# A selective-scan kernel: six of 48 drive products a step move to GpSimd, fed by DMA-broadcast B rows

## The reference, cut to what matters

```python
xs, z = split(h @ in_w)                       # 192 channels each
xc = silu(causal_conv4(xs) + conv_b)
dt, Bm, Cm = split(xc @ xproj_w)              # 6, 16 and 16 columns
delta = softplus(dt @ dt_w + dt_b)
dA  = exp(delta[..., None] * A)               # 16 states per channel
dBx = delta[..., None] * Bm[:, :, None, :] * xc[..., None]
h_t = dA_t * h_{t-1} + dBx_t                  # scan over the 4096 tokens
y = (einsum('blds,bls->bld', h, Cm) + Dp * xc) * silu(z)
seq = seq + y @ out_w
```

## Time and profile before

| | |
|---|---|
| median of 3 runs | 4664.84 us (4664.05 to 4667.70) |
| the profiled execution: its time, its span | 4665.67 us, 4663.9 us |
| first and last scan start (L600, 1536 of them) | 68.6 and 3117.8 us |
| DVE, PE, ACT, POOL busy | 3569.4, 4156.8, 2405.1, 2479.7 us |

### The profile page before, as it was taken

How to read it: one execution, slowest core, us unless ns; L and a number is a source line. 1 busy time by engine, 2 the same in 40 slices (tenths; PEclk the granted TensorE clock), 3 DMA queues, 4 the chain that set the end, 5 groups by cost and what they waited for, 6 DMA issues and landing times. The chain is left out here.

```text
span 4663.9 us, 44769 instructions
## 1 busy us (share of the span) xinstructions
PE 4156.8 (89%) x13922; PEld 1791.2 (38%) x13922; DVE 3569.4 (77%) x4331; ACT 2405.1 (52%) x3937; POOL 2479.7 (53%) x1991
## 2 busy tenths in 40 slices
PE   7999999999999999999999999863989888988964
PEld 2333333333333333333333333221546555655543
DVE  4999999999999999999999999976015415414345
ACT  5666667666666667666666666632012312312223
POOL 4778877888778877888778877761000000000000
PEclk8999999999999999999999999996999999999976
DMA  3444444444444444444444444433010010000000
GB/s 94 131 131 139 135 143 135 137 136 145 135 135 138 133 145 137 136 136 142 136 134 139 137 138 135 127 115 100 12 42 18 18 43 17 18 15 4 18 1 14
DMA packets 135434, 459.67 MB, mean 99 GB/s; under 512 B 20623, under 2 KB 23122, under 8 KB 133662
## 3 DMA queue, kind: packets, MB, share of 16 engines
q1 hardware_dynamic: 135198, 456.82, 32.0%
HBM read 431.28 MB, written 20.97 MB: 97 GB/s over the span
## 5 line engine op out<-in xcount | busy, mean ns | idle before, releaser
L668 POOL TENSOR_TENSOR prod<-states,c_rows 128x512 f32<-128x512 f32 x1536 | 1935.9, 1274 | 591.5 <-DVE states L600 575.7
L600 DVE TENSOR_TENSOR_SCAN states<-decay,carry,bpsum 128x512 f32<-128x512 f32 x1536 | 1937.6, 1262 | 0.0
L357 PE MATMUL ypsum<-prod,identity 128*128 128x512 f32 x3072 | 1587.8, 598 | 0.4 <-POOL prod L668 0.3
L459 ACT ACTIVATE decay<-delta,decay_rate 128x512 f32<-128x512 f32 x1536 | 1078.4, 716 | 722.3 <-DVE states L600 623.6
L587 DVE TENSOR_TENSOR bpsum<-bpsum,dx 128x512 f32<-128x512 f32 x1536 | 1034.8, 674 | 89.9 <-PE bpsum L350 71.7
L350 PE MATMUL bpsum<-b_rows,select 96*128 96x512 bf16 x1536 | 595.4, 388 | 163.7 <-DVE states L600 162.1
L357 PEld LDWEIGHTS ypsum<-prod,identity 128*128 128x128 f32 x3072 | 592.0, 194 | 311.3 <-issue 176.3
L350 PEld LDWEIGHTS bpsum<-b_rows,select 96*128 96x128 bf16 x1536 | 147.9, 96 | 1068.1 <-DVE states L600 666.2
L1073 PE MATMUL convp<-img_hi,w_hi 96*96 96x512 f16 (+1 forms) x1568 | 483.4, 385 | 65.1 <-PEq L1476 49.0
L1434 DVE SCALAR_TENSOR_TENSOR x<-convp,unscale,x_group 96x1024 f32<-96x1024 f32 x16 | 20.4, 1278 | 406.3 <-PE convp L1073 406.3
L1073 PE MATMUL convp<-img_hi,w_lo 128*96 128x512 f16 (+1 forms) x896 | 276.3, 388 | 0.0
(11 more groups left out here) (215 smaller groups left out, 4526.2 us busy)
## 6 DMA issues: line engine op xcount, KB each, us to landing
c_rows<-c_map SPq DMA_DIRECT2D x512, 512.0 KB, 3.7
c_rows<-c_map SPq DMA_DIRECT2D x512, 256.0 KB, 3.9
x_in<-in_x SPq DMA_DIRECT2D x16, 384.0 KB, 6.0
fused_map<-fused SPq DMA_DIRECT2D x16, 384.0 KB, 5.1
work<-fused_map SPq DMA_DIRECT2D x4, 1536.0 KB, 9.8
x<-in_x SPq DMA_DIRECT2D x4, 1536.0 KB, 16.1
x_biased_map<-work SPq DMA_DIRECT2D x4, 1536.0 KB, 7.1
x_group<-x_biased_map SPq DMA_DIRECT2D x16, 384.0 KB, 3.7
```

The source lines that it names most:

```text
L357: pe.matmul(ypsum[:, group % Y_BANKS, :], identity[:, :], prod[:, n % P_RING, :], start=s == 0, stop=s == STATES - 1).then_inc(summed, 1)
L459: act.activation(decay[:, n % RING, :], delta[k % 2][:, g, :], ACT.Exp, scale=decay_rate[:, ORDER[k][0], g, s:s + 1]).then_inc(decay_ready, 1)
L600: dve.tensor_tensor_scan(states[:, n % H_RING, :], decay[:, n % RING, :], bpsum[:, n % B_BANKS, :], carry[:, at, u:u + 1], ALU.mult, ALU.a ...
L668: pool.tensor_tensor(prod[:, n % P_RING, :], states[:, n % H_RING, :], c_rows[:, n // C_STATES % C_RING, n % C_STATES, :], ALU.mult).then_ ...
```

## The change

Six units of each step, 19, 23, 27, 31, 35 and 47, are *pooled*. For them there is no PE broadcast and no DVE scale. The B row, stored in f32 in DRAM beside C, is broadcast by a DMA on SP's queue into a ring of two SBUF buffers (`b_wide`); POOL multiplies it by dx into `drive` (two buffers) in the slot two before the unit; ACT writes the decay of that unit into the PSUM bank that the broadcast would have used, three slots ahead; the scan takes its factor from PSUM and its addend from `drive`. The projection is one chain of three matmuls (B once, C, dt). The split is made on 32 rows, and mid and low are moved to their rows of `b_rows` by two DMAs on SP. Several due slots move forward; one buffer of softplus (`tmp2`) becomes single.

```diff
+POOL_UNITS, POOL_LEAD, B_RING = (19, 23, 27, 31, 35, 47), 2, 2
 EARLY:
-    "proj": [30, 31, 32, 33, 34, 35], "hi": [35, 36], "rest": [37], "mid": [38], "low": [39],
-    "dt": [37, 40, 41], "v": [38, 41, 42], "soft": [39, 40, 41, 42, 43, 44],
+    "proj": [30, 31, 32], "hi": [33], "rest": [35], "mid": [36], "low": [37],
+    "dt": [34, 38, 36], "v": [35, 39, 37], "soft": [36, 37, 38, 39, 40, 41],
-SP_AT = 8
+SP_AT, SP_ROWS_AT, SP_MOVE_AT = 8, 17, 18
...
 SP:
+                def load_b(i):
+                    k, u = divmod(pool_unit(i), STEP_UNITS)
+                    g, s = divmod(u, STATES)
+                    if i % POOLED == 0:
+                        sp.wait_ge(rows_stored, 16 * (k + 1))
+                    if i >= B_RING:
+                        sp.wait_ge(driven, i - B_RING + 1)
+                    broadcast_rows(0, k, g, s, 1, b_wide[:, i % B_RING, :], b_loaded[i % B_RING])
+                def move_b(step):
+                    sp.wait_ge(mid_ready, step + 1)
+                    sp.dma_start(b_rows[step % 2][BC_ROWS:2 * BC_ROWS, :], b_mid[:, :]).then_inc(b_moved, 16)
+                    sp.wait_ge(bank0_read, USE[0, step - 1, PROJ] + 1)
+                    sp.dma_start(b_rows[step % 2][2 * BC_ROWS:, :], b_low[:, :]).then_inc(b_moved, 16)
...
+                        if at == SP_ROWS_AT and w + 1 < STEPS:
+                            store_rows(w + 1)
+                        if at == SP_MOVE_AT and w + 1 < STEPS:
+                            move_b(w + 1)
                         if i < STEPS * C_LOADS:
                             load_c(i)
+                        while next_b < POOLED * STEPS and (pool_unit(next_b - B_RING) + 3) // 2 <= C_LOADS * w + at:
+                            load_b(next_b)
+                            next_b += 1
 PE:
-                        pe.wait_ge(bank0_read, USE[0, k - 1, PROJ] + 1)
+                        pe.wait_ge(hi_ready, k + 1)
+                        pe.wait_ge(b_moved, 32 * (k + 1))
...
-                    if 0 <= t + B_LEAD < UNITS:
+                    if 0 <= t + B_LEAD < UNITS and not on_pool(t + B_LEAD):
                         broadcast_b(t + B_LEAD)
 ACT:
+                    if on_pool(n):
+                        if n >= B_BANKS:
+                            act.wait_ge(scanned, n - B_BANKS + 1)
+                        into, done = bpsum[:, n % B_BANKS, :], wide_ready
 DVE:
+                    if on_pool(n):
+                        dve.wait_ge(driven, i + 1)
+                        dve.wait_ge(wide_ready, i + 1)
+                        by, add = bank, drive[:, i % B_RING, :]
...
-                    if 0 <= t + 1 < UNITS:
+                    if 0 <= t + 1 < UNITS and not on_pool(t + 1):
                         scale_unit(t + 1)
 POOL:
+                def drive_unit(n):
+                    k, u = divmod(n, STEP_UNITS)
+                    g, i = u // STATES, pooled_before(n)
+                    if i >= B_RING:
+                        pool.wait_ge(scanned, pool_unit(i - B_RING) + 1)
+                    pool.wait_ge(dx_ready, 3 * k + g + 1)
+                    pool.wait_ge(b_loaded[i % B_RING], 16 * b_landings(i))
+                    pool.tensor_tensor(drive[:, i % B_RING, :], b_wide[:, i % B_RING, :], dx[k % 2][:, g, :],
+                                       ALU.mult).then_inc(driven, 1)
...
+                    if 0 <= t + POOL_LEAD < UNITS and on_pool(t + POOL_LEAD):
+                        drive_unit(t + POOL_LEAD)
                     if 0 <= t < UNITS:
                         unit(t)
```

More of the change, by code:

```diff
@@ L36 @@
 DT_AT = SPLITS * BC_ROWS
+C_FROM, DT_ROW = DT_AT + 2 * RANK, 2 * BC_ROWS
 EPS = 1e-5
@@ L64 @@
     "z2": [25, 26], "z2_copy": [27], "z01": [27, 28], "z01_copy": [28, 29], "silu_z": [31],
[L65 to L66 removed]
+    "proj": [29, 30, 31], "hi": [32], "rest": [34], "mid": [35], "low": [36],
+    "dt": [33, 37, 35], "v": [34, 38, 36], "soft": [35, 36, 37, 38, 39, 40],
 }
@@ L109, with on_pool, pooled_before, pool_unit @@
 USE = bank_uses()
+def on_pool(n):
+    return n % STEP_UNITS in POOL_UNITS
+def pooled_before(n):
+    k, u = divmod(n, STEP_UNITS)
+    return POOLED * k + sum(at < u for at in POOL_UNITS)
+def pool_unit(i):
+    return STEP_UNITS * (i // POOLED) + POOL_UNITS[i % POOLED]
+OTHERS = [n for n in range(UNITS) if not on_pool(n)]
+def others(n):
+    return n - pooled_before(n)
+def b_landings(load):
+    return sum(2 if POOL_UNITS[i % POOLED] >= 2 * STATES else 1 for i in range(load % B_RING, load + 1, B_RING))
 def c_landings(load):
@@ L289, in load_x, with broadcast_rows @@
                                  dram["x"][:, 2 * pair:2 * pair + 2, c * CHUNK:c * CHUNK + CHUNK]).then_inc(x_loaded[pair], 16)
+                def broadcast_rows(kind, k, g, first, count, tile, loaded):
+                    for r0, r1, b in (((0, 128, 0),), ((0, 128, 1),), ((0, HALF, 0), (HALF, 128, 1)))[g]:
+                        rows = bc_dram[k % 2, kind, b, first:first + count, :].rearrange("s n -> (s n)")
+                        sp.dma_start(tile[r0:r1], rows.unsqueeze(0).to_broadcast([r1 - r0, count * CHUNK])).then_inc(loaded, 16)
                 def load_c(i):
@@ L318, in finish @@
                         load_x(pair, c + 1)
-                store_c(0)
+                store_rows(0)
+                move_b(0)
                 for i in range(C_RING):
                     load_c(i)
+                for i in range(B_RING):
+                    load_b(i)
+                next_b = B_RING
                 for w in range(STEPS):
@@ L456, in unit @@
                         act.wait_ge(delta_ready, 3 * k + g + 1)
[L457 to L460, removed]
+                    if on_pool(n):
+                        if n >= B_BANKS:
+                            act.wait_ge(scanned, n - B_BANKS + 1)
+                        into, done = bpsum[:, n % B_BANKS, :], wide_ready
+                    else:
+                        if others(n) >= RING:
+                            act.wait_ge(scanned, OTHERS[others(n) - RING] + 1)
+                        into, done = decay[:, others(n) % RING, :], decay_ready
+                    act.activation(into, delta[k % 2][:, g, :], ACT.Exp,
+                                   scale=decay_rate[:, ORDER[k][0], g, s:s + 1]).then_inc(done, 1)
                 def save_carry(n):
@@ L565, in _ @@
                     w, at, coming, done, current = now(t)
-                    if 0 <= t + DECAY_LEAD < UNITS:
+                    if 0 <= t + B_LEAD < UNITS and on_pool(t + B_LEAD):
+                        unit(t + B_LEAD)
+                    if 0 <= t + DECAY_LEAD < UNITS and not on_pool(t + DECAY_LEAD):
                         unit(t + DECAY_LEAD)
```

117 lines of the change are left out of this document (62 added, 55 removed).

## The result

The changed kernel takes 4836.83 us (median; 4834.54 to 4838.04) against 4665.32 us before: ratio 1.0363, interval 1.035 to 1.0375. That is 171 us slower. The forecast was slower by 97 us, with a range that ended at 4825: the sign and the place are right, the size is too small and the range missed.

The account below looks back on a forecast made before the run. DVE and PE were both near full, DVE setting the pace. Per step 92.1 - 3.5 (scales) + 0.85 (unit 19) + 8.4 (late B rows) = 97.9 us against 94.86; +3.0 over 32 steps gave 4762 us, range 4685 to 4825.

Parts of the forecast that it names:

- DVE's saving of 3.5 us a step: On DVE, six scales a step removed at 0.58 us each, counted as on the path.
- PE's waits: DVE's waits for PE's broadcasts late in the step, about 2.7 us, expected to vanish inside the drive waits.
- a surplus of 6.3 us: PE's work over DVE's in the loaded stretch, now ending at slot 32: 6.3 us, as before, so PE waits alone would stay.
- The swapped operands of the scan: In pooled units' scans, factor from PSUM and addend from SBUF: taken as 0, with +-0.6 us a step kept.
- Rival 3: Every drive on POOL also holds DVE up; three cost 1.27 us each a step on top: 4885 us; chance 0.02.
- L: Time from the releasing product's end to the B row's landing: 4.4, 5.0, 5.3 us for units 27, 31, 35; sum 14.7.
- these 256 KB rows are nearest: C-load rows of the same size, source and queue, landing 3.9 us after issue in the median, taken for the B copies.
- My walk: Timeline of landings, drives and products from product 23 to scan 35, which starts 8.4 us late.
- Units 19 and 47: DVE waits 0.85 us at unit 19, where POOL still works off softplus; no wait was counted at unit 47.
- My bounds: Landing at the shortest, 3.3 us, gives 4704; as much above the median gives 4820; the scan widens each end by 19.
- Rival 1: B rows land in 2.1 us like the 192 KB stores: -2.1 us a step, 4597 us; chance 0.12.
- my formula: Change per step = sum of the three L minus 11.65 us.

Follow-up runs that it names:

- e1: Against the changed kernel, the B loads of units 27, 31 and 35 are issued two SP iterations (four products) sooner; 4647.43 us, ratio 0.996.
- e9: Against e1, the B loads of units 27, 31 and 35 come one SP iteration sooner than in the change, not two; 4649.13 us, ratio 0.9958.
- e10: Against e7, all B loads are released as late as in the change, so four rows are late; 4948.13 us, ratio 1.0599.
- e3: Against the changed kernel, no pooled units; single projection chain, split by DMA and sooner softplus stay; 4662.77 us, ratio 0.9995.
- e7: Against e6, pooled units at 21, 25, 29, 33, 37, 41, with the sixth unit's B rows also loaded early; 4581.90 us, ratio 0.9808.
- e2: Against the changed kernel, B loads issued ahead of the C load of their SP iteration, released by the same product; 4678.64 us, ratio 1.0027.
- e4: Against the changed kernel, three more f32 matmuls, result unused, in PE's slot 35 where PE stood still; 4812.33 us, ratio 1.0311.
- e6: Against the changed kernel, e1's early loads, projection spread over slots 30, 32, 34 with later split, softplus in 39 to 44; 4643.34 us, ratio 0.9935.

## Why the prediction was right or wrong

**Right, and shown.** The B rows of units 27, 31 and 35 are late, because SP releases them one product before POOL wants them (e1, e9 and e10 move the time with the release alone). The waits grow from unit to unit, unit 23 waits for nothing, DVE's saving of 3.5 us a step is real and is overrun. The prediction expected PE's waits to be gone, and they are not: 47.5 us of 71.7 over the run are left, nearly all of them at the scales of units 28 to 32. But there DVE would wait for the next drive anyway, so they cost nothing on top, which is what the sum had assumed. That PE's relief alone is worth nothing was forecast too (a surplus of 6.3 us before and after). e3 shows it for the three matmuls, and in e1, with the broadcasts gone as well, DVE still waits 3.8 us a step for PE; the expectation for e3, which gave it 35 to 85 us, forgot what the prediction had counted: the deadline comes sooner by as much. The swapped operands of the scan cost nothing (1280 against 1264 ns). Rival 3, the port: the products still take 1277 ns and the scans 1264 beside them, as before; no run shows the shared port costing anything here, and the Trainium skill's warning that moving work between GpSimd and DVE might not help ("Perfetto Trace Analysis", "Optimizing Scalar/DVE Operations") did not come true in e7, which has the same six products on POOL and is 1.9% faster.

**Wrong: the size.** The step has 11.6 us of DVE idle where I summed 9.25, and 2.4 us x 32 is 77 us, against the 75 by which the forecast fell short. By the terms of the sum:

- *L, the term that decided.* I took 3.9 us for the 256 KB copy and 3.7 for the halves, from the C rows. In the trace, as means over 25 steps, these copies landed 4.5, 4.3 and 4.1 us after their issue, and L is 4.9, 5.4 and 5.9 us, 16.2 in sum against 14.7: 1.5 us a step, 48 of the 75 us. The step that failed is "these 256 KB rows are nearest": those C rows had at most one neighbour of their size ahead, the B rows have 512 KB, and in e2, without these, the same copies land 0.4 to 0.6 us sooner. I priced the SP issue ahead of the B load and not the bytes ahead of it.
- *From landing to drive, put at nothing.* My walk starts a drive when its row lands. In the trace it starts 0.16 us later, three times a step: 0.5 us. These two terms cover the stretch from unit 27 to 35, where DVE's idle is 1.27 + 3.28 + 4.43 + 1.25 (scales) = 10.2 us against the 8.4 of my walk.
- *Units 19 and 47*: 1.13 us against 0.85, and 0.27 against nothing.
- *The clock, which I did not have.* I wrote that PE catches up in the pauses. It does, but after the longest one at half its clock. e4 prices this at 0.77 us a step, in unit 47's wait and in the stretch above, so it is a part of those numbers and not on top of them.
- *The range did not follow from its own terms.* My bounds were 4704 to 4820, widened by 19 at each end for the scan's new form: 4685 to 4839. The range has the lower end of that and stops at 4825 above. The wider end would have held 4836.83, but by luck: the new form costs 16 ns, six times a step, which is 0.1 us where 0.6 was allowed for, and the time came from the terms above.

**The rule of the Trainium skill.** By its fit of 2.0 us plus bytes over 436 GB/s ("DMA: Bandwidth & Descriptors", "Anatomy of one DMA") I had put 256 KB at 2.6 us and the time at 4635. The page gives that fit for DMAs issued by GpSimd, and these are issued by SP. The traces show 4.3 us behind C loads and 3.8 with the B load first (medians); the measurement decides. Rival 1, of the same kind, is refuted for this kernel; its point of decision, a mean L of 3.9 us, is borne out by e2, which has just that mean (11.7 in sum) and lands 13 us above the kernel before, where my formula says 2 above.

**Also wrong, in an expectation:** that early rows would give 4570 to 4610 us. With the wait of 9 us gone, waits of 5.3 us a step are left. Unit 19's 1.1 us was there before and PE's at the scales (2.8 us) had been hidden, and the expectation counted both; it had no wait for rest (1.0 us) and none for unit 47 (0.4 us). DVE's work outside the waits is also 89.3 us a step where it took 88.6.

**Open.** Two things stay without a cause: why e4's gain stands mostly at units 27 to 35, and what beside the bytes ahead sets a landing (3.8 to 5.1 us in e1 for the rows of units 27, 31 and 35). e7 also had no stretch of slow clock in these steps where e6 had 3.5 us of it a step; its gain is accounted for by the waits, but no run separates the two.

## What to carry to other kernels

When work moves to an engine that is fed by DMA, write down for each transfer the event that releases it and the instruction that wants it, both as positions in the in-order lists: if fewer operations lie between them than the landing takes, the transfer's latency becomes the pace, once for every such item. A load should be released by what frees its buffer, not by a later beat that happens to drive the queue: here the buffer was free seven products before the release (products 17 to 23 for unit 27). Put the small urgent load ahead of the large lazy one; and put offloaded work where the receiving engine has caught up, since it waits for everything queued before it.

## What the runs showed of the hardware that I had not expected

A pause of 3.3 to 4.9 us in PE, after a stretch of continuous work, went with a granted clock of 0.50 in each of 25 steps of the changed kernel; the slow clock lasted 7 to 20 us, 11.7 in the mean, most of it behind the pause. With three extra matmuls in the pause the time at 0.50 fell from 11.7 to 2.1 us a step, and the kernel is 24.5 us faster for the added work. The landing of a 128 KB copy varied between 2.9 us (e2) and 4.0 us (the change) in the median, with the C bytes ahead of it in the change and behind it in e2; a copy of 256 KB took 3.8 us in e2.
